# One product of the state-space layer with 128 weight columns, 96 of them zero, in place of 32

## The reference, cut to what matters

```python
dt = jax.nn.softplus(dt + dt_bias)          # per token and head, 8 heads
A = -jnp.exp(A_log)
dA = dtc * A                                 # the decay increments
dA_cs = jnp.cumsum(dA, axis=2)               # their running sum over the chunk
diff = dA_cs[:, :, :, None, :] - dA_cs[:, :, None, :, :]
Lmat = jnp.where(causal, jnp.exp(diff), 0.0)
y_off = jnp.einsum('bcihn,bcih,bchpn->bcihp', Cc, jnp.exp(dA_cs), prev_states)
```

## Time and profile before

| | |
|---|---|
| median of 3 runs | 2198.18 us (2197.79 to 2201.4) |
| span of the profiled execution | 2195.2 us |
| its own time beside the span | not given; the median is 2.98 us above the span |
| TensorE products busy | 2138.3 us, 97% |
| weight loads | 1781.6 us, 81% |
| VectorE, ScalarE, GpSimd busy | 1761.4, 1750.8, 1682.2 us (80%, 80%, 77%) |
| mean granted TensorE clock | 0.992 of full speed |

### The profile page before, as it was taken

How to read it: one execution, slowest core, us unless ns; L and a number is a source line. 1 busy time by engine, 2 the same in 40 slices (tenths; PEclk the granted TensorE clock), 3 DMA queues, 4 the chain that set the end, 5 groups by cost and what they waited for, 6 DMA issues and landing times.

```text
span 2195.2 us, 51248 instructions
## 1 busy us (share of the span) xinstructions
PE 2138.3 (97%) x16090; PEld 1781.6 (81%) x16090; DVE 1761.4 (80%) x4001; ACT 1750.8 (80%) x4402; POOL 1682.2 (77%) x1812
## 2 busy tenths in 40 slices
PE   6799999999999999999999999999999999999997
PEld 5678888888888888888888888888888888888875
DVE  7778778887778888788888788888788887788863
ACT  5788887888887888888888888888888888888872
POOL 3568787777787777787777787777787777787786
PEclk9899999999999999999999999999999999999998
DMA  4221222222222222222222222222212222222210
GB/s 138 88 78 52 83 62 66 88 79 64 83 62 67 88 79 63 83 62 67 88 75 67 83 62 67 88 74 68 83 62 67 88 70 72 80 65 67 78 56 20
DMA packets 152204, 161.03 MB, mean 73 GB/s; under 512 B 15128, under 2 KB 134528, under 8 KB 151936
## 3 DMA queue, kind: packets, MB, share of 16 engines
q1 hardware_dynamic: 150160, 157.63, 23.4%
q10 hardware_dynamic: 1776, 0.12, 0.1%
HBM read 139.88 MB, written 17.83 MB: 72 GB/s over the span
## 4 chain that ended last, share of the span: by engine, by line
PE 89%; issue 3%; POOL 3%; DVE 3%; ACT 2%; DMA 0%; POOLq 0%; SPq 0%; DVEq 0%; ACTq 0%
PE pe L1320 32%; PE pa L1320 22%; PE pd L1320 12%; PE px L1320 10%; PE py L1320 6%; PE px L1432 3%; PE pa L1338 1%; PE pd L1491 1%; DVE feat L933 1%; PE py L1423 1%; POOL xd L423 0%; POOL ex L474 0%; POOL ex L479 0%; POOL ex L485 0%; POOL ex L470 0%
## 5 line engine op out<-in xcount | busy, mean ns | idle before, releaser
L933 DVE SCALAR_TENSOR_TENSOR feat<-pa,cw,feat 128x512 f32<-128x512 f32 x567 | 423.8, 747 | 83.5 <-ACT feat L609 73.1
L1320 PE MATMUL pe<-e_hi,h_hi 128*128 128x512 f32 x1024 | 443.7, 433 | 3.7 <-DVE eacc L1124 2.0
L1320 PE MATMUL pe<-e_lo,h_hi 128*128 128x512 f32 x1024 | 405.2, 396 | 0.0
L1320 PE MATMUL pe<-e_hi,h_lo 128*128 128x512 f32 x1024 | 404.4, 395 | 0.0
L1320 PE MATMUL pa<-h_hi,w_hi 128*128 128x260 f32 x1260 | 371.8, 295 | 6.3 <-DVE feat L933 5.7
L1320 PE MATMUL pa<-h_hi,w_lo 128*128 128x260 f32 x1260 | 357.8, 284 | 0.0
L1320 PE MATMUL pa<-h_lo,w_hi 128*128 128x260 f32 x1260 | 357.0, 283 | 0.0
L681 ACT ACTIVATE lm<-lm,lndt 128x128 f32<-128x128 f32 x1024 | 329.7, 405 | 2.5
L671 ACT ACTIVATE lm<-lm,e3in 128x128 f32<-128x128 f32 x1024 | 324.6, 405 | 1.1 <-DMA lm<-cs_rows 1.1
L761 ACT ACTIVATE ex<-pe,wg 128x256 f32<-128x256 f32 x512 | 215.0, 478 | 114.7 <-PE pe L1320 93.1
L1124 DVE SCALAR_TENSOR_TENSOR eacc<-pe,wg,eacc 128x256 f32<-128x256 f32 x512 | 244.3, 477 | 31.8 <-PE pe L1320 22.8
(11 more groups left out here) (184 smaller groups left out, 5659.3 us busy)
## 6 DMA issues: line engine op xcount, KB each, us to landing
lm<-cs_rows SPq DMA_DIRECT2D x128, 512.0 KB, 4.0
ebc<-cs_rows SPq DMA_DIRECT2D x256, 128.0 KB, 3.6
xin<-_attn_hidden_states_dram SPq DMA_DIRECT2D x32, 512.0 KB, 5.1
xres<-_attn_hidden_states_dram SPq DMA_DIRECT2D x128, 128.0 KB, 3.7
out_dram<-x SPq DMA_DIRECT2D x128, 128.0 KB, 3.9
gz<-in_L_wmod_dram SPq DMA_DIRECT2D x2, 512.0 KB, 8.2
ex<-in_L_ffn_expert_w_dram SPq DMA_DIRECT2D x1, 1024.0 KB, 11.5
x<-in_L_ffn_expert_w_dram SPq DMA_DIRECT2D x1, 1024.0 KB, 13.9
```

Source lines behind the costliest of these rows:

```text
L933: dve.scalar_tensor_tensor(out=acc, in0=proj_bank(x, i)[:, :, 1 + j:1 + j + HT], scalar=cw[:, f, j:j + 1], in1=acc, op0=ALU.mult, op1=ALU. ...
L1320: return pe.matmul(o, lhsT=l, rhs=r, start=start, stop=stop, skip_group_check=True)
```

## The change

The increments now stand in columns 32 to 63 of a zeroed 128 by 128 tile. The two products that take them as moving operand read the same 32 columns; the third takes the whole tile as weights, so that its result covers all 128 partitions of the bank, with the wanted rows on partitions 32 to 63 as before and zeros elsewhere. A memset on GpSimd zeroes the tile once, and VectorE waits for it before its first write.

```diff
-        dA = sb("dA", [P, T, NH])
+        dA_pad = sb("dA_pad", [P, P])
+        dA = dA_pad[:, 32:32 + T * NH].rearrange("p (t h) -> p t h", h=NH)
...
             pool.memset(wgate[:, :, NE:32], 0.0).then_inc(POOL0.sem, 1)
+            pool.memset(dA_pad[:], 0.0).then_inc(POOL0.sem, 1)
             pool.memset(ident[:], 0.0).then_inc(POOL0.sem, 1)
...
                     dve.wait_ge(DVE0.sem, DVE0.at["a_rep"])
-                dve.tensor_tensor(dA[:], dt[:], rep(a_rep[:], T, NH), ALU.mult).then_inc(S["dts"], 1)
+                    dve.wait_ge(POOL0.sem, POOL0.at["zdA"])
+                dve.tensor_tensor(dA, dt[:], rep(a_rep[:], T, NH), ALU.mult).then_inc(S["dts"], 1)
...
-                flat = dA[:].rearrange("p t h -> p (t h)")
+                flat = dA_pad[:, cs_rows]
                 mm_(pa[:, 0, 0:T * NH], tri[:], flat, True, True)
                 mm_(pa[:, 0, T * NH:2 * T * NH], all_ones, flat, True, True)
-                mm_(pa[cs_rows, 1, 0:P], flat, tri[:], True, True).then_inc(S["cs"], 1)
+                mm_(pa[:, 1, 0:P], dA_pad[:], tri[:], True, True).then_inc(S["cs"], 1)
```

More of the change, by code:

```diff
@@ L193, in __init__ @@
                 self.at = {step: i + 1 for i, step in enumerate(steps)}
-        POOL0 = Steps("pool_0", ["zdt", "zgate", "z_ident", "ident", "neghalf", "eps", "zero", "o_tri", "tri", "s0", "s1", "bz"]
+        POOL0 = Steps("pool_0", ["zdt", "zgate", "zdA", "z_ident", "ident", "neghalf", "eps", "zero", "o_tri", "tri", "s0", "s1", "bz"]
                       + [f"elo{i}" for i in range(4)])
```

## The result

| | |
|---|---|
| before | 2198.37 us, median of 21 runs (2196.16 to 2201.4) |
| changed | 2201.12 us, median of 21 runs (2199.66 to 2205.33) |
| ratio | 1.0015, 95% interval 1.0009 to 1.0021 |

The change made the kernel slower by 0.15%, some 3 us. The forecast of 2197.2 us was 3.9 us off, and the result lies 0.6 us above the range. It is a loss where a small gain was forecast.

What follows compares the result with a forecast made beforehand. TensorE was taken to bound the kernel. Gains of 0.8 us (30 groups), 0.12 (group 1) and 0.1 (group 0) made 1.0 off the 2195.2 us span; 2194.2 plus 2.98 for the runs' median gave 2197.2, range 2192.5 to 2200.5.

Steps and rivals of the forecast that it cites:

- The other parts, costed at nothing: GpSimd's memset, the write of dA with its new wait, and VectorE's earlier read of px: 0 us in the sum.
- The rival on the slow side: At cs_, pauses stay and two wider weight loads add 0.16 us per group, 5.1 us slower, 2203.2 us; chance 0.05.
- (c): Behind px, ft3 waits for ScalarE's csTe, so only 0.02 to 0.03 us per group is gained: 0.8 us over 30.
- (a): On TensorE from the last dA,tri to px's second pass, 0.75 us becomes 0.44: 0.31 us removed per group.
- (b): Two weight loads of 128 columns instead of 32, 0.08 us more each, counted as nothing; at most 0.16 us per group.
- Group 1: There ScalarE's L657 waited for cs, which ends 0.12 us earlier; gain counted 0.12 us, bounds 0.12 and 0.31.
- What can be told from no change: Whole-kernel threshold: differences up to about 0.2% (4.4 us) count as no change; chance of landing within it 0.82.
- The memset: GpSimd at the start, 0.20 us ahead of ident; hidden because TensorE's first transpose waits for a transfer; counted as nothing.
- What the profile would show: Around cs_: 190 ns loads, pitch 0.11, px in 1.06, ft3 paused some 0.29 us, listed as 6 to 9 us ScalarE waits.

Runs made afterwards that it cites:

- e1: Kernel before, narrow product kept, with an unused 384-byte tensor behind dA that moves everything allocated after it: ratio 1.0024, 29 periods +5.3 us.
- e2: Changed kernel with dA_pad allocated last and an unused tensor in dA's old place, so other tensors keep their addresses: ratio 0.9994, 29 periods -0.6 us against before.
- e11: Changed kernel with 128 more unused bytes behind dA_pad, so everything behind is shifted by 512: ratio 0.9990, 29 periods -1.1 us against before.
- e3: e2 with the wait for csTe moved from the head of ft3 to its second half: ratio 0.9970, 29 periods -6.8 us against before.
- e14: Kernel before with only wo_hi and wo_lo moved by 128 bytes, all else in its old place modulo 256: ratio 1.0014, 29 periods +5.4 us.
- e6: Kernel before with 384 unused bytes ahead of y_hi instead of behind dA: ratio 1.0014, 29 periods +4.2 us.
- e9: Kernel before with an unused gap of 64 bytes per partition behind dA: ratio 1.0026, 29 periods +6.4 us.
- e12: Kernel before with an unused gap of 192 bytes per partition behind dA: ratio 1.0031, 29 periods +8.7 us.
- e7: Kernel before with an unused gap of 256 bytes per partition behind dA: ratio 1.0001, 29 periods -0.1 us.
- e8: Kernel before with an unused gap of 512 bytes per partition behind dA: ratio 1.0001, 29 periods -0.2 us.
- e17: Kernel before with only h2_hi and h2_lo moved by 128 bytes, all else in its old place modulo 256: ratio 1.0005, 29 periods +1.7 us.

## Why the prediction was wrong, point by point

- **The failed step** is a term that the sum did not have. "The other parts, costed at nothing" listed the memset, the write and wait of `dA`, and the earlier read of `px`, and left out the first line of the diff, which makes an allocation larger and so moves all behind it by 384 bytes. That term, at nothing in the sum, measured +5.3 us alone (e1). With the local -0.76 it gives +4.5, and +4.5 was measured. The rival on the slow side (the pause stays and the loads show, 0.05) named a loss of 5.1 us, near that size, for a reason that is wrong: e2 has the wide loads and loses nothing. The cause was in none of the cases, for which the prediction had kept 0.02.
- **(c) `ft3` held by `csTe`, 0.025 us per group kept:** right, 0.026 over the 29 periods, and with the address undone the kernel is 1.1 us (e11) or 0.6 us (e2) faster there, against 0.7 forecast for 29 periods. e3 shows the hold by lifting it.
- **(a) 0.31 us removed at `cs_`:** mis-sized. All pitches were to be 0.11. In the changed kernel, from the last `dA,tri` (1345.17 + 0.53 - 0.28 = 1345.42) to the second pass of `px` (1345.95) are 0.53 us, not 0.44, since the two passes of the padded product start 0.19 apart (1345.53 + 0.47 - 0.28 = 1345.72). So 0.22 is removed and the pause is 0.19, not 0.29. It did not matter here, as the wait swallowed it, but it is why e3 gained less than I expected.
- **(b) wider loads at nothing:** right but for that 0.08 us between the two passes. It may be the wider load's share, which no run separates; hidden here, it is in e3's result. The Trainium skill's page TensorEngine Tiling (Array Packing), section Key Properties, says that a change of tiling mode drains the engine; this trace agrees in that the pauses at the way in and the way out are gone. By the starts, the one narrow product cost 0.22 us more than the padded one.
- **Group 1:** `ft3`'s load stands at 93.62, the first `dA` product at 92.09: 1.53 us where the kernel before has 94.05 - 92.29 = 1.76. It gained 0.23, within the bounds of 0.12 and 0.31, but not by the term of the sum: ScalarE got 0.04 and not 0.12 (its reader starts 93.03 - 92.09 = 0.94 behind the first `dA` product, before 93.27 - 92.29 = 0.98), because of the 0.08 of (a). The load stands 0.01 behind the last pass of `px` (92.83 + 1.06 - 0.28 = 93.61), so it took the whole 0.22 and did not wait for ScalarE.
- **What can be told from no change:** the prediction took 0.2% (4.4 us) for it. With 21 runs of each kernel the interval is 0.06% to either side, so 0.15% is a loss and not scatter.
- **The memset** has 0.20 us at 0.94, and TensorE's first transpose still waits for its transfer: right.
- **What the profile would show:** right for the loads, the 1.06 of `px`, L659 behind L763 and the load behind L660. Wrong for the table of waits: it has no entry of ScalarE for `ft3`, though the pause is there in the starts, because the weight loads and the modelled ends of products overlap it. I had written that I am wrong if that wait is absent; the test was badly chosen, and e3 is the one that decides. The pause is 0.19 us and not the 0.29 said, by (a).

## What to carry to other kernels

A diff that changes the size of an on-chip tensor moves everything allocated behind it: look there first when code that was not touched slows down by a few per cent, and hold the addresses fixed (allocate last, or pad to the same place modulo 256 bytes) before judging an edit worth less than 0.5%. Measure such things over a long run of equal periods within one trace, where kernels that differ only in a move without effect agreed to 0.2 us in 1915, and not by spans, which differed by several. And where a gain is swallowed by a wait for the reader of a buffer, see which part of the buffer is really read: here the wait moved down by half a step and gave 6 us, but only after the edit that by itself gave 1.

## What the runs showed of the hardware

- Where tensors stand on chip changes the time of products, and not only of those that read them (e14, e1 against e6), with no view of waits showing it. Everything behind `dA` moved by 64, 192 or 384 bytes per partition cost 6.4, 8.7 and 5.3 us in 1915, and up to 0.3% of the whole kernel (e9, e12); moved by 256 or 512 bytes it cost nothing (e7, e8). In the block shown, the output projection's passes (256 columns, the reduced float format) start 113 ns apart before, 118 with 384 and 119 with 64.
- In the kernel before and the changed one a block of such passes keeps to some 113 or some 118 ns from start to start once it is under way, and its own addresses do not settle which. Equal blocks of neighbouring groups take 1.18 and 1.14 us in turn in the kernel before, and 1.13 and 1.17 in e17.
- One product with 32 weight columns between products with 128 takes 0.22 us more than the same product padded to 128 columns.
- TensorE's pause of 0.19 us ahead of `ft3`, which the later wait takes away (e3), has no entry in the table of waits.
